# SyncE instead of GpSimd waits for a ring slot's release in a two-layer graph network kernel

## The reference, cut to what matters

```python
# layer 0: attention over the edges
w = jnp.sum(q[s] * k[d], axis=1) / d_k
ew = jnp.exp(w - wmax[d])
alpha = ew / denom[d]
out = jax.ops.segment_sum(alpha[:, None] * x[s], d, num_segments=N)
# layer 1: weighted sum over the edges
gathered = support[edge_col] * edge_val[:, None]
out = jax.ops.segment_sum(gathered, edge_row, num_segments=x.shape[0])
```

## Time and profile before

| | us |
|---|---|
| median of the runs | 6699.03 |
| span of the profiled execution | 9414.7 |
| stretch with the gat gathers, profiled | 1590 to 4392 |
| stretch with the gcn gathers, profiled | 6647 to 8962 |
| stretch from there to the end, profiled | 8962 to 9415 |

### The profile page before, as it was taken

The page is one execution under the profiler, slowest core; times in us unless marked ns, Lnnn a source line. Parts: engine busy times, 40 slices in busy tenths (PEclk is TensorE's granted clock), DMA queues, the critical chain, the costliest instruction groups (busy, mean ns, idle before and its releaser), DMA issues. The chain is left out here.

```text
span 9414.7 us, 116831 instructions
## 1 busy us (share of the span) xinstructions
PE 5293.0 (56%) x22154; PEld 3875.0 (41%) x22155; DVE 3692.5 (39%) x14368; ACT 1980.3 (21%) x4706; POOL 4691.2 (50%) x5589
## 2 busy tenths in 40 slices
PE   0431176777777777786055371089444444444479
PEld 0320154555555555554044360078333333333367
DVE  6340154444444445555143240046333333333345
ACT  6110043333333333333011120023000000000034
POOL 3476501555555555554725427600566666666600
PEclk9775577888888888887577685599777777777789
DMA  2100000333333333332000000000233333333300
GB/s 78 28 4 3 5 1 22 89 86 85 83 84 80 78 81 82 78 80 78 3 1 3 2 19 5 5 7 1 70 91 90 91 91 91 90 91 90 91 27 18
DMA packets 505062, 495.27 MB, mean 53 GB/s; under 512 B 374733, under 2 KB 401878, under 8 KB 504150
## 3 DMA queue, kind: packets, MB, share of 16 engines
q0 software_dynamic: 200192, 432.72, 16.8%
q1 hardware_dynamic: 154712, 33.52, 2.0%
q10 hardware_dynamic: 150013, 27.32, 1.7%
HBM read 462.90 MB, written 30.23 MB: 52 GB/s over the span
## 5 line engine op out<-in xcount | busy, mean ns | idle before, releaser
L1794 POOL DMA_INDIRECT XN<-table,XN x3128 | 2980.2, 953 | 990.0 <-issue 934.5
L557 POOL DMA_INDIRECT records<-slot_rec,slot_pos x1564 | 1532.7, 980 | 598.5 <-issue 598.5
L2098 PE MATMUL gcn_psE<-XN,gcn_pE 128*125 x3520 | 1120.2, 482 | 1218.7 <-DVE gcn_pE L2114 911.1
L75 POOL TENSOR_TENSOR cell<-cell 1x1 int32<-1x1 int32 x874 | 164.1, 188 | 2674.5 <-DMA XN<-records 967.0
L2098 PEld LDWEIGHTS gcn_psE<-XN,gcn_pE 128*125 128x125 f32 x3520 | 823.5, 243 | 1515.3 <-issue 1354.9
L1923 PE MATMUL gat_psE<-XN,gat_pE 128*125 x3520 | 1046.0, 448 | 253.9 <-issue 173.3
L1923 PEld LDWEIGHTS gat_psE<-XN,gat_pE 128*125 128x125 f32 x3520 | 738.9, 221 | 397.1 <-issue 277.9
L2126 DVE TENSOR_TENSOR X<-X,gcn_psE 125x256 f32 x440 | 184.3, 419 | 1538.6 <-remote 1063.1
L1907 PE MATMUL gat_psS<-XN,gat_kTs 25*125 25x512 f32 x880 | 579.4, 742 | 181.3 <-ACT XN L1952 162.3
L2114 DVE TENSOR_SCALAR gcn_pE<-iota_n,gcn_lk,gcn_rec 128x125 f32<-128x125 f32 x1760 | 501.4, 363 | 16.0
L2180 ACT ACT_TABLE_LOAD x1 | 1.3, 1283 | 2345.4 <-PEq L117 2345.4
(11 more groups left out here) (453 smaller groups left out, 8451.4 us busy)
## 6 DMA issues: line engine op xcount, KB each, us to landing
XN<-table,XN POOLq DMA_INDIRECT x3128
records<-slot_rec,slot_pos POOLq DMA_INDIRECT x1564
XN<-records SPq DMA_DIRECT2D x782, 6.0 KB
gat_rec<-records ACTq DMA_DIRECT2D x440, 6.0 KB
gcn_rec<-records ACTq DMA_DIRECT2D x440, 6.0 KB
table<-XN ACTq DMA_DIRECT2D x5, 1250.0 KB
table<-room ACTq DMA_DIRECT2D x25, 250.0 KB
out_x<-X SPq DMA_DIRECT2D x25, 250.0 KB
```

The costliest lines, as they stand in the source:

```text
L557: pool.indirect_dma_start(out=rec_d[1], out_offset=bass.IndirectOffsetOnAxis(ap=slot_pos[:, h, j:j + 1], axis=0), in_=slot_rec[:, h, j, :] ...
L1794: pool.indirect_dma_start(out=rows_t[:, s, j, :], out_offset=None, in_=table, in_offset=bass.IndirectOffsetOnAxis(ap=rec_g[:, s, j, 1:2].b ...
L2098: last = pe.matmul(psE[d][0:B, 0:D], pE[:, d, j, :], rows_t[:, slot_of(g), j, :].rearrange("p a w -> p (a w)"), start=(j == 0), stop=(j == ...
```

## The change

SyncE gets the read of `first_step` and the wait on `used`, ahead of its record load for every group but the first eight; GpSimd loses both. The same code serves both edge stages. The slot's records are thus loaded only once the slot is free, and GpSimd knows it free because the records are there. The signal to `arrived` of group g - 4 stays behind the load of g in SyncE's order.

```diff
                 def body(t, s):
+
+                    if not (isinstance(t, int) and t == 0):
+                        n = sp.value_load(first_step[which][0:1, bass.ds((t - 1) * RING + s + 1, 1)], min_val=1, max_val=NS)
+                        sp.wait_ge(used, n)
                     load_records(sp, t * RING + s, rec_g[:, s, :, :], group_ready[s])
                     if near(t, s, -LAG):
                         arrive(*near(t, s, -LAG))
@@
                     pool.wait_ge(group_ready[s], t * 16 + 16)
-                    if not (isinstance(t, int) and t == 0):
-
-                        n = pool.value_load(first_step[which][0:1, bass.ds((t - 1) * RING + s + 1, 1)], min_val=1, max_val=NS)
-                        pool.wait_ge(used, n)
                     settle(pool, cell[0:1, 0:1], settled, t * RING + s)
```

## The result

The changed kernel takes 7643.24 us (7637.82 to 7656.28), the one before 6698.62: 1.141 times as long, with a 95% interval of 1.1396 to 1.1424. The forecast was slower by 442 us, 7140 us with a range up to 7410. The direction and the place were right, and the size was not: it is 944 us.

The account below looks back on a forecast made before the run. GpSimd's pitch of 5.07 us a group was taken to bound both edge stages. After the change gat takes 240 x 7.05 + 200 x 4.10 = 2512 us against 2070, so 6699 + 441 = 7140 us, range 6860 to 7410.

Parts of the forecast that it names:

- What bounds the kernel before: Both edge stages run at GpSimd's pace, 5.07 us a group; waits for TensorE's sums (449 us) belong mostly to recording.
- gat before, 2070 us: Plain gat stage of the kernel before: between 1982 and about 2150 us, taken as 2070, not the 2802 profiled.
- GpSimd's read and wait worth nothing: Removing GpSimd's read and wait gains 0, hidden behind queued gathers; at most 337 us if that cover were gone.
- The records' later load worth nothing: Loading records only after the slot's release costs 0 as long as consumers lag fewer than three groups.
- gcn at no cost: In gcn, announcing group x + 4 only after TensorE finishes group x is no limit: cost 0.
- The loop over take_q: In gat, sums, SyncE's signal, take_q, exp and the next sums form a closed loop; the change costs 442 us (chance 0.75).
- 240 turns, 200 steps at 4.10 us: Of gat's 440 steps, 240 are turns of the loop; the other 200 run at TensorE's serial 4.10 us.
- A turn at full clock, 6.45 us: One loop turn in gat, from sums through SyncE and take_q to the next sums: 6.45 us without a clock drop.
- The clock, one gap in three: About one in three of TensorE's 2.20 us gaps drops its clock, adding 1.70 us: turns average 7.05 us.
- The range's top, 7410 us: Every gap in gat drops the clock, turns at 8.15 us: gat 2776 less 2070, so 7405, rounded to 7410.
- The rival in which the clock stays low (0.10): In gat TensorE's clock does not recover: turns towards 10.55 us, 7980 us in all, half way 7650; chance 0.10.
- Two of my signs for telling right from wrong: In the changed trace's gat, take_q waits for SyncE in some 240 steps; GpSimd's add waits for record DMA, not gat_psE.

Follow-up runs that it names:

- signal_first_b: Changed kernel with SyncE's signal of group g - 4 moved ahead of its wait for slot g, on a first-kind chip: 6700.66 us, ratio 1.000.
- both_wait: Changed kernel with GpSimd's read and wait put back beside SyncE's: 7652.13 us, 1.142 times the kernel before.
- lag_three: Changed kernel with LAG = 3 instead of 4, so the signal of g - 3 stands behind the load of g: 6700.84 us, ratio 1.000.
- gap_filled: Changed kernel with ten extra transposes per step on TensorE ahead of its wait for the exp: 7380.22 us, 1.102 times the kernel before.

## Why the prediction was right and wrong

- **What bounds the kernel before: right, by a wrong reason and so by luck.** GpSimd's pitch of 5.07 us a group, taken as real, gives 1982 us for a stage; gat has 2002 and gcn 1991 with their starts and ends. But the reason given, that recording had stretched the rest, was wrong. GpSimd happens to be the engine whose instructions are the same on both kinds, and the median and the trace were of different kinds. A span beside a median can't tell the two apart. The 449 us of the earlier trace rows were not the recording's either.
- **gat before, 2070 us: 68 too high.** The middle of the bounds was taken, where the floor itself was right. The upper bound had a slip too: 0.98 + 0.30 us for a scatter is 1.28, not 1.26, which makes 2002 us and not 1971, and about 2120 the bound for gat, not 2150. The 68 us are part of the 499 by which the forecast for gat's growth (442 of 941 us) fell short.
- **GpSimd's read and wait worth nothing: shown** by signal_first_b at the kernel before's time and both_wait at the changed kernel's.
- **The records' later load worth nothing: shown** by signal_first_b and lag_three.
- **gcn at no cost: right on the chips timed**, and not on the other kind.
- **The loop over take_q: shown.** lag_three moves one constant and takes the whole loss away.
- **240 turns, 200 steps at 4.10 us: right.** They are 4.11 us in the changed kernel.
- **A turn at full clock, 6.45 us: nearly right.** It is 6.26: 0.77 us from sums to take_q where I had summed 0.90, and 5.49 us from there, where I read 5.55 in the earlier trace rows.
- **The clock, one gap in three: this is the step that failed.** A turn has 8.72 us where I had 7.05. I had put the price of a drop at 1.70 us and its chance at a third, some 0.60 us a turn, 144 us in all. gap_filled shows 2.46 us a turn on average, 590 us. Both factors were too small: all but 9 of the turns sorted are slow, and a slow one has 8.84 us where a full-clock one has 6.30, 2.54 more. The price came from a gap that had only the sums and the weights behind it; here the gap stands ahead of all of a step's matmuls, and the slow stretch meets scores, turn and sums. 240 x (8.72 - 7.05) = 401 us, and with the 68 above and some 30 that these means leave over that is the 499.
- **The range's top, 7410 us**, had every gap drop the clock and was still short, since it kept the price of 1.70 us and took 2070 us for gat before.
- **The rival in which the clock stays low (0.10)** was nearer in size than the forecast: of the 4.10 us that it adds to a turn 2.46 came. That its "half way", 7650 us, is nearly the measured time is luck. Half way between turns of 6.45 and 10.55 us is 8.50, and by the prediction's own sum that gives 7489 us. Nor does the clock stay low: in the turns shown it is back at 1.00 ahead of the next weights, and falls again behind them.

The rule that I weighed from the Trainium skill, page "TensorE: Matmul & The Clock Gate", section "HAM oscillation — how this bites in real kernels", says that bursts parted by waits start slow each time. Its waits are of some 3 to 5 us, so carrying it over to gaps of 2 us was my step and not the page's. The traces here agree with it in the outcome, at gaps of 1.9 us: clock 0.78 over gat, and a slow stretch behind nearly every gap. They differ in the detail: the burst shown starts at full speed and slows down from its scores on. I had one row that agreed with the outcome, and gave it a third; it deserved to be the forecast.

Two of my signs for telling right from wrong were worth less than I thought. take_q waits for SyncE 239 times in the kernel before too, since a consumer that keeps up with GpSimd always waits for the last gather; the total, 636 against 1463 us, tells them apart and the count doesn't. And that GpSimd's add would no longer wait for gat_psE says little: on the first kind of chip GpSimd waited 9 us for it in gat before. SyncE's own wait, 2381 us in gat, was the sign that told.

## What to carry to other kernels

When a wait moves to an in-order engine, list everything that engine does for others behind it: here a one-word signal stood behind a slot's release, and eight slots of ring became four groups of lead. Then count how far ahead the furthest reader looks, here three steps: with a lead of four groups the group that it wants for the very next step is announced only at the end of the last one, the pipeline closes into a loop, and the loop's length, not the throughput of any engine, is the pace. With a lead of five it doesn't. And price the loop with the clock that its idle gaps leave, not with the clock of the busy trace it is read from.

## What the runs showed of the hardware

- TensorE's clock in a repeating pattern of work and gap: with gaps of 1.91 us and 4.1 us of work (at full clock) the granted clock is 0.78 over the stage, and turns have 8.72 us instead of 6.26. In the turn shown the clock is 1.00 through the gap and the weights, and 0.50 from then on. With gaps of 1.38 us about a quarter of the turns stay at full clock. With 0.82 us left by the filled gap it is 0.95, and in the kernel before, with 0.64 to 0.78 us in the steps looked at, 0.99.
- Work that nobody needs can pay: 4400 transposes, 1.25 us for ten, made the kernel 267 us faster.
- From the end of a matmul that releases SyncE, over its record load's issue and one signal, to ScalarE's start: 0.77 us. Without the load's issue it is 0.24 us, so issuing a DMA of 6 KB holds SyncE for 0.53 us.
- The same program takes 6700 us on at least two chips and 9410 on another, each within 0.3% of its median; all engines but GpSimd have instructions near 0.7 us on the latter. The cause stays open.
